# Attention layer and a gated feed-forward on one core: tiles 16 to 31 of the inner dimension computed in pairs by seven half products

## What is computed

```python
x = x + attn(layernorm(x), Wq, bq, Wk, bk, Wv, bv, Wbeta, bbeta, Walpha, balpha)
Wg, Wu, Wd = (dequant_nvfp4(W_packed, scales) for gate, up, down)      # [4096, 512] x2, [512, 4096]
gate = einsum('th,nh->tn', layernorm(x), Wg)
up   = einsum('th,nh->tn', layernorm(x), Wu)
out  = einsum('tn,hn->th', gelu_tanh(gate) * up, Wd)
x = x + out
```

## Time and profile before

| | us |
|---|---|
| median of 3 runs (lowest, highest) | 1156.45 (1156.41, 1156.68) |
| the profiled execution: its time | 1156.49 |
| the profiled execution: its span | 1154.7 |
| TensorE busy | 1148.6 (99%) |
| VectorE busy | 720.1 (62%) |
| GpSimd busy | 508.0 (44%) |
| ScalarE busy | 426.7 (37%) |

### The profile page before, as it was taken

One profiled execution on the slowest core, in us unless ns is written; L12 is line 12 of the kernel. 1 busy time (PEld: TensorE's weight loads), 2 busy tenths in 40 slices (PEclk: granted clock), 3 DMA queues, 4 the chain that ended last, 5 costly groups with the idle time before them and its releaser, 6 DMA issues.

```text
span 1154.7 us, 19336 instructions
## 1 busy us (share of the span) xinstructions
PE 1148.6 (99%) x7788; PEld 760.9 (66%) x7788; DVE 720.1 (62%) x1239; ACT 426.7 (37%) x975; POOL 508.0 (44%) x503
## 2 busy tenths in 40 slices
PE   9999999999999999999999999999999999999998
PEld 5666655565444445777777777777777777777775
DVE  7788656365675855665666566655665566565333
ACT  4343334252233233343434343434343434343332
POOL 2386535133256744344635363536353635363110
PEclk9999999999999999999999999999999999999999
DMA  8021111000110010110011001100110011000011
GB/s 298 5 75 38 37 37 37 10 10 1 35 57 1 19 37 19 38 37 20 19 37 37 20 19 37 38 19 19 38 37 20 21 38 34 22 24 21 37 38 64
DMA packets 22680, 41.92 MB, mean 36 GB/s; under 512 B 2688, under 2 KB 2752, under 8 KB 22592
## 3 DMA queue, kind: packets, MB, share of 16 engines
q1 hardware_dynamic: 22592, 40.70, 11.0%
...
## 4 chain that ended last, share of the span: by engine, by line
PE 97%; DVE 1%; POOL 0%; issue 0%; ACT 0%; POOLq 0%; DVEq 0%; ACTq 0%
PE ps L468 38%; PE ps L502 29%; PE ps L429 14%; PE ps L336 9%; PE ps L302 1%; PE ps L390 1%; PE ps L373 1%; PE ps L397 1%; PE ps L384 1%; PE ps L364 1%; PE ps L509 0%; DVE XT L834 0%; DVE bigA L828 0%; PE ps L312 0%; POOL WR L1246 0%
## 5 line engine op out<-in xcount | busy, mean ns | idle before, releaser
L502 PE MATMUL ps<-WR,ihl_s 128*128 128x512 f16 x768 | 183.4, 379 | 0.0
L502 PE MATMUL ps<-WR,vv 128*128 128x512 f16 x720 | 172.5, 379 | 0.0
L429 PE MATMUL ps<-XT,WR 128*128 128x512 f16 x768 | 170.3, 379 | 0.0
L468 PE MATMUL ps<-XT,WR 128*128 128x256 f16 x1152 | 157.1, 273 | 0.0
L468 PE MATMUL ps<-REG,WR 128*128 128x256 f16 x1152 | 157.1, 273 | 0.0
L1027 DVE TENSOR_TENSOR load<-load,ps 128x256 f32<-128x256 f32 x144 | 60.7, 422 | 144.5 <-PE ps L468 93.2
L468 PEld LDWEIGHTS ps<-REG,WR 128*128 128x128 f16 x1152 | 112.7, 98 | 33.5
L429 PEld LDWEIGHTS ps<-XT,WR 128*128 128x128 f16 x768 | 75.0, 98 | 90.0 <-DVE fw L953 0.5
L723 ACT COPY load<-ps 128x256 f32<-128x256 f32 x144 | 53.6, 372 | 211.1 <-PE ps L468 211.1
L1246 POOL TENSOR_TENSOR WR<-wf,WR 128x512 f16<-128x512 f32 x48 | 58.8, 1245 | 154.3 <-ACT WR L673 154.3
L468 PEld LDWEIGHTS ps<-XT,WR 128*128 128x128 f16 x1152 | 112.7, 98 | 13.3
...
## 6 DMA issues: line engine op xcount, KB each, us to landing
...
```

The lines of the kernel that those rows point to most:

```text
L429: mm = eng.matmul(bank[:, :], buf[:, wp, o + kt, 128 * j:128 * j + 128], XT[:, xp, kt, 512 * b:512 * b + 512], start=(n == 0), stop=(n == 11))
L468: mm = eng.matmul(half_bank(kind, name), w(wp, kt), x(xp, kt), start=(first and n == 0), stop=(n == 5), skip_group_check=True)
L502: mm = eng.matmul(PS[bank][:, :], ih[:, ip, 128 * tt:128 * tt + 128], buf[:, wp, 8 + j, :], start=(j == 0 and p == 0), stop=(j == end and ...
```

## The change

- Tiles 16 to 31 (pairs 8 to 15) are computed by `products` too; `upgate` ends with tile 15.
- Group 1 therefore gets weight sums: chunks 7 and 9 get difference, chain and splits during tiles 11 to 15. Chunks 6 to 9 are all worked off before pair 8, chunks 10 and 11 in pairs 8 and 9, and later ones in the pair that they had relative to their group.
- The token sums of block 0 are made before tile 11, those of blocks 1, 2 and 3 around pairs 8, 10 and 12. The four sets of `R` stand in four places: free slots of `WR1`, key columns of `REG`, and two sets in slots of `WR0` that are read out.
- The low halves of tiles 12 to 14 move from GpSimd to VectorE, those of tiles 16 to 31 to GpSimd.
- Even and odd groups swap the places of their gate sums; the second load slot is given up from chunk 10 on (it was from 12).

```diff
 def nth(i):
 
-    return i + 1 if i < 32 else (i ^ 1) + 1
+    return i + 1 if i < 16 else (i ^ 1) + 1
 
 
 def on_pool(i):
-    return 8 <= i < 15 and i != 11 or 32 <= i < NI - 2
+    return 8 <= i < 11 or 16 <= i < NI - 2
...
-    return 32 + 3 * (m - 16) + PIECES[name]
+    return 16 + 3 * (m - 8) + PIECES[name]
...
-        R = [two(bigB[:, 512 * j:512 * j + 512]) for j in range(4)]
...
-            return XT[:, a, 0:2, 512 * j + 256:512 * j + 512] if g % 2 else GX[j][a]
+            return GX[j][a] if g % 2 else XT[:, a, 0:2, 512 * j + 256:512 * j + 512]
...
+        def sums_in(buf, at):
+            return [buf[:, q // 2, at + 2 * (q % 2):at + 2 * (q % 2) + 2, :].bitcast(F32) for q in range(4)]
+
+        R = [sums_in(WR1, 8), [two(REG[:, 1, 1, 512 * q:512 * q + 512]) for q in range(4)],
+             sums_in(WR0, 4), sums_in(WR0, 8)]
...
-                if m == 16:
-                    pe.wait_ge(s_inter, 32)
+                if m == 8:
+                    pe.wait_ge(s_inter, 15 if kind == "gate" else 16)
...
                 product("P1", left(0, e0), toks(0, 0))
-                if m > 16:
+                if m > 8:
                     pe.wait_ge(s_comb, pair_base(kind, m - 1, 3) + COMBINED["C12"])
                 product("P5", left(0, o0), sums(0))
+                if m == 8:
+                    pe.wait_ge(s_inter, 16)
                 product("P2", left(2, e0), toks(2, 0))
...
-            for i in range(NT - APART, 32):
+            for i in range(NT - APART, 16):
                 upgate(i)
                 if i == 11:
                     turn("n2", NT - 1)
@@ -560,10 +567,8 @@
                 if i == 12:
                     for tt in range(4):
                         down(2, tt)
-                if i >= 16:
-                    down(i // 4 - 1, i % 4)
             banks.ring = [6, 7]
-            for m in range(16, NI // 2):
+            for m in range(8, NI // 2):
...
             def dq_first(k):
                 base, buf = k % 6 * 2, WR[k // 6 % 2]
                 ac.wait_ge(s_dq, 6 * k + 6)
-                ac.wait_ge(s_dn, 16 * (k // 6 - 1))
+                if k == 6:
+                    ac.wait_ge(s_mm["v"], 16)
+                elif k == 8:
+                    ac.wait_ge(s_dn, 12)
+                else:
+                    ac.wait_ge(s_dn, 16 * (k // 6 - 1))
+                if k == 14:
+                    ac.wait_ge(s_tlo, 12)
...
             def token_sums(b):
                 ac.wait_ge(s_T, 4 * b + 4)
                 ac.wait_ge(s_yg, 12)
+                if b == 3:
+                    ac.wait_ge(s_tlo, 8)
                 for t, q in enumerate((0, 3, 1, 2)):
-                    eng.copy(TB[b][:, 0, t], R[q]).then_inc(s_thi, 1)
+                    eng.copy(TB[b][:, 0, t], R[b][q]).then_inc(s_thi, 1)
...
-                    ac.wait_ge(s_tlo, 16)
-                    ac.wait_ge(s_dq, 72)
+                if m == 8:
+                    if kind == "gate":
+                        ac.wait_ge(s_dq, 60)
+                    else:
+                        ac.wait_ge(s_yl, NT)
+                        ac.wait_ge(s_dl, 12)
...
-            act_tile(NT - APART)
-            act_tile(NT - APART + 1)
+            act_tile(10)
+            dequant(6)
+            act_tile(11)
             turn("n2", NT - 1)
-            dequant(6)
-            for i in range(12, 32):
-                act_tile(i)
-                if i in (12, 13, 14, 16, 18):
-                    dequant({12: 7, 13: 8, 14: 9, 16: 10, 18: 11}[i])
-                if 16 <= i < 24 and i % 2:
-                    token_sums((i - 16) // 2)
-                if i in (25, 31):
-                    dq_sums(13 if i == 25 else 15)
-                elif i >= 20 and i % 2:
-                    dequant({21: 12, 23: 13, 27: 14, 29: 15}[i])
-            dk = 16
-            for m in range(16, NI // 2):
+            token_sums(0)
+            dequant(7)
+            dq_sums(7, 0, 2)
+            act_tile(12)
+            dq_sums(7, 2, 4)
+            dequant(8)
+            dequant(9)
+            act_tile(13)
+            dq_sums(9, 0, 2)
+            act_tile(14)
+            dq_sums(9, 2, 4)
+            act_tile(15)
+            dk = 10
+            for m in range(8, NI // 2):
...
+                if m in (8, 10, 12):
+                    token_sums(m // 2 - 3)
...
                 dv.wait_ge(s_dq, 6 * k + 4)
                 if paired and k % 2:
                     dv.wait_ge(s_wlo, wlo_count(k - 1, 0))
-                    if k == 13:
+                    if k == 7:
...
-            def token_sums(b):
+            def token_sums(b, first=0, last=4):
                 dv.wait_ge(s_R, 4 * b + 4)
-                for n, (out, x, y) in enumerate(((0, 1, 0), (1, 3, 1), (3, 3, 0), (2, 2, 3))):
+                steps = ((0, 1, 0), (1, 3, 1), (3, 3, 0), (2, 2, 3))
+                for n, (out, x, y) in list(enumerate(steps))[first:last]:
                     if n:
                         dv.wait_ge(s_T, 4 * b + n)
-                    eng.tensor_tensor(R[out], R[x], R[y], ALU.subtract).then_inc(s_T, 1)
+                    eng.tensor_tensor(R[b][out], R[b][x], R[b][y], ALU.subtract).then_inc(s_T, 1)
...
+            dq_bits(6)
             apply("n2", NT - 1)
-            act_tile(NT - APART)
-            act_tile(NT - APART + 1)
+            dq_finish(6)
+            act_tile(10)
+            token_sums(0)
+            dq_bits(7)
+            act_tile(11)
             turn_low("n2", NT - 1)
+            dq_finish(7)
             gather(1, 2)
             gather(1, 3)
-            dq_bits(6)
-            dq_finish(6)
-            for i in range(12, 32):
-                if i == 12:
-                    dq_bits(7)
+            dq_bits(8)
+            act_tile(12)
+            for tt in range(3):
+                gather(2, tt)
+            dq_finish(8)
+            dq_bits(9)
+            gather(2, 3)
+            dq_finish(9)
+            for i in range(13, 16):
                 act_tile(i)
-                if i == 12:
-                    for tt in range(4):
-                        gather(2, tt)
-                    dq_finish(7)
-                    dq_bits(8)
-                if i == 13:
-                    dq_finish(8)
-                    dq_bits(9)
-                if i == 14:
-                    dq_finish(9)
-                if i == 15:
-                    dq_bits(10)
-                if i == 16:
-                    dq_finish(10)
-                if i == 17:
-                    dq_bits(11)
-                if i == 18:
-                    dq_finish(11)
-                if 16 <= i < 24 and i % 2:
-                    token_sums((i - 16) // 2)
-                if i in (21, 23, 27, 29):
-                    k = {21: 12, 23: 13, 27: 14, 29: 15}[i]
-                    dq_bits(k)
-                    dq_finish(k)
-                if i >= 16:
-                    gather(i // 4 - 1, i % 4)
-            dk = 16
-            for m in range(16, NI // 2):
+            dk = 10
+            for m in range(8, NI // 2):
...
                 combine("gate", m, "C22")
+                if m in (8, 10, 12):
+                    token_sums(m // 2 - 3, 0, 2)
                 combine("gate", m, "C12")
                 gather(n, 2 * m % 4)
                 if bits:
                     dq_sign(dk)
+                if m in (8, 10, 12):
+                    token_sums(m // 2 - 3, 2, 3)
                 combine("up", m, "C11")
                 if m % 8 not in (4, 7) and dk < 48:
                     dq_finish(dk)
                     dk += 1
+                if m in (8, 10, 12):
+                    token_sums(m // 2 - 3, 3, 4)
                 combine("up", m, "C22")
...
             def dq_difference(k):
-                if k == 13:
-                    pl.wait_ge(s_tlo, 16)
-                pl.wait_ge(s_dq, 6 * k + 6)
+                if k == 7:
+                    pl.wait_ge(s_attn, NT)
...
                 pl.wait_ge(s_chain, at + 1)
+                pl.wait_ge(s_dq, 6 * k + 6)
                 eng.tensor_tensor(a21, a21, a22, ALU.add).then_inc(s_chain, 1)
...
-                pl.wait_ge(s_yl, NT)
-                pl.wait_ge(s_attn, NT)
-                if b:
-                    pl.wait_ge(s_tlo, 4 * b)
+                if b == 0:
+                    pl.wait_ge(s_mm["v"], NT)
+                elif b == 1:
+                    pl.wait_ge(s_attn, NT)
+                elif b == 2:
+                    pl.wait_ge(s_gu["up"], 16)
+                else:
+                    pl.wait_ge(s_dn, 16)
                 for q, (k, o) in enumerate(quad):
                     hi, lo = (XT[:, a, k:k + 2, 512 * b + o:512 * b + o + 256] for a in range(2))
-                    eng.tensor_tensor(R[q], hi, lo, ALU.add).then_inc(s_R, 1)
+                    eng.tensor_tensor(R[b][q], hi, lo, ALU.add).then_inc(s_R, 1)
...
-            inter_low(NT - APART + 1)
+            token_sums(0)
+            inter_low(10)
             dequant(6)
-            for i in range(12, 32):
```

(43 more changed lines are left out.)

45 lines of the change are left out of this document (24 added, 21 removed).

## The result

The changed kernel takes 1159.05 us (median of 12 runs, 1158.82 to 1159.5) against 1156.49 us (1156.32 to 1156.88) of the kernel before in the same rounds: ratio 1.0022, interval 1.0014 to 1.0029. It is slower by 2.6 us: little, but the interval leaves out no change. The profiled spans differ by as much, 1157.2 against 1154.7.

The account below looks back on a forecast made before the run. The prediction took TensorE's own work, busy 99% of the span, to bound the kernel. Its terms, -9.5 + 9.3 + 0.6 + 1.6 = +2.0 us on 1156.49, gave 1158.5 us, range 1149.5 to 1163 (likeliest case 1155.5 to 1161).

Parts of the forecast that it names:

- TensorE's work, -9.5: Tiles 16 to 31: eight pairs of half products replace plain tiles, 16 x (7.77 - 7.175) = 9.5 us less on TensorE.
- rival of binding weight loads: Half matmuls: each brings its own 98 ns load, so a slower pitch undoes the gain, up to 1168 us; chance 0.02.
- To `upgate(12)`, 4.7: Before tile 12: TensorE waits 4.7 us for `turn_low`, as `upgate(12)` starts at 301.5 in place of 296.85.
- seven meetings of 0.85 us: VectorE's list before `upgate(12)`: seven instructions that read only SBUF are each held 0.85 us by GpSimd, 6.0 us together.
- To the second P3 of pair 8, 9.3 in all: Pair 8: block 1's additions end at 343.9, up's C22 at 350.9; total lateness 9.3 us, including the 4.7 before.
- Pair 9, 0.6: Start of pair 9: ScalarE's token and weight copies delay the first snapshot, so TensorE gets it 0.6 us late.
- rival of inherited lateness: Pairs 9, 10 and 12: GpSimd's late lows cost 2 to 3 us each, 1162 to 1165 us; chance 0.18.
- Pairs 10 and 11, nothing: Pair 10: 2.8 us of token differences fit VectorE's gaps, costing nothing; pair 11 was given no price of its own.
- Pair 12, 1.6: Pair 12: four differences beside GpSimd cost 4 x 1.5, partly absorbed by idle time and reserve; 1.6 us, bounds 0 and 3.
- its signs: Changed profile: TensorE waits of 10 to 12 us between 296 and 400, block 1's additions ending near 344, none past pair 13.
- Half is paid back: Up to pair 12: fewer than half of the meetings happen, lateness 5 to 6 us; 1151 to 1154 us; chance 0.26.
- No meeting: Up to pair 8: VectorE and GpSimd never hold each other, `upgate(12)` starts in time; 1147 us; chance 0.09.

Follow-up runs that it names:

- the best version: Changed kernel with block 0's sums and chunk 6 in the attention stage, chunk 7 ahead of tile 11, chunk 14's bits in pair 13; also called the last version: 1149.29 us.
- the filler run: Changed kernel with 19 extra matmuls of 512 columns, their result overwritten, filling TensorE's wait ahead of `upgate(12)`: 1158.99 us.
- the moved versions: Changed kernel with `turn_low` moved earlier (1158.18 us), or block 0's sums and chunk 6 moved into the attention stage (1153.04 us), also with chunk 7 earlier (1151.83 us).

## Why the prediction was right, step by step

**TensorE's work, -9.5.** Right: 109.2 ns for each half matmul in the new pairs too, and the best version shows 9.1 us less busy time. The rival of binding weight loads has nothing for it. The estimate of 15 us more, worked out from the sustained figures of the Trainium skill (TensorE: Matmul & The Clock Gate, Back-to-back issue gap), is not borne out.

**To `upgate(12)`, 4.7.** Measured 4.15. I had counted seven meetings of 0.85 us, 6.0 in all. The rows show apply +0.8, finish +1.9, differences +2.6 and 0.45 of waiting for the additions, 5.8. They fell on other instructions than I had named (the bits of chunk 6, which end as GpSimd begins, kept the lengths they have alone). The clock's fall behind this wait, 1.6 us, I had not foreseen; the filler run shows that it costs nothing here, since pair 8 is late anyway. The other stop on the way, `inter(13)` behind `dq_finish(9)`, which was to hold `upgate(15)` or the start of pair 8 by about 1 us, holds nothing in this trace. It shows only where the slow clock is gone (0.37 and 0.39 us) or the wait at `upgate(12)` (3.88 us).

**To the second P3 of pair 8, 9.3 in all.** Measured 7.5. The direction and the place are right: VectorE's first difference of block 1 waits (2.94 us), the up half's C22 is what TensorE waits for, and taking 3 us out of the series takes 3 off the time. The size is off: the additions end at 342.55 and not at 343.9, and from there to P3 it is 6.6 us, where the prediction had 7.0 (343.9 to 350.9). Of the 1.35 us, 0.5 is there at its first token low (300.65 against 301.2), and 0.2 is a slip in its sum: 301.2 and 5.3 make 306.5, not 306.7.

**Pair 9, 0.6.** The snapshot is 0.55 us late, as said. Another 0.8 at this pair's P3 I had not priced. ScalarE's and VectorE's timelines of the changed kernel:

```profile
358.49 0.42 ACT L647 ACTIVATE fw<-load 128x256 f32<-128x256 f32 x1 [2.99 <-POOL ihl_s L1245]
```

```profile
361.62 2.87 DVE L1036 SCALAR_TENSOR_TENSOR wf<-tb,load 128x512 f32<-128x512 f16 x2
```

GELU of tile 19 waits for GpSimd's low of tile 17, behind the token lows, just as the rival of inherited lateness had it, but that is not what holds P3. VectorE, whose C22 releases it, works without a pause from the gate's C12 (357.73) to that C22 (364.41). It is late by its own instructions beside GpSimd's lows and additions of block 2: 1.13, 1.53 and 2.87 us, where rows 5 have 0.42, 0.69 and 1.29. The wait is also still there, 0.64 us, in the last version, whose pair 8 waits for nothing. So the prediction left out, in this pair, the very price that it had counted up to pair 8.

**Pairs 10 and 11, nothing.** Measured 0.35 and 0.45: small, but wrong. Pair 11 is like pair 9, with a finish of 2.87 us beside the additions of block 3; when these move to pair 10, its wait goes. Pair 10's is a `down` that waits for GpSimd's low of a tile, behind the additions of block 2.

**Pair 12, 1.6.** Measured 2.25. Its differences took 3.11, 1.64 and 1.30 us, together the 4 x 1.5 of the prediction; the idle time into which I let 1.8 us fall was partly taken by `dq_bits`, held by GpSimd as well. The one-line edit that moves those bits away ends the wait.

So the mechanism was right where it was large, but the sum came out as near as it did by luck: 1.8 us too much up to pair 8 and 2.2 too little behind it cancel. Of its signs, the end of the additions and pairs 9 and 12 came near; the waits came lower, 7.0 us from 296 to 400 and 1.9 behind that, where it asked for 10 to 12 up to 400. The slow clock and smaller gaps make up the rest of the 11.9. No wait goes on past pair 12. "Half is paid back" had the meetings cheaper than in the rows of before; they were not. "No meeting" needed `upgate(12)` on time, which only the moved versions reach.

What stays open: whether the 0.6 us in the attention stage and the 0.65 us at pair 9 can go without a new wait. Neither was tried.
